# A graph layer and an LSTM on one core: the first stage with its products one line behind, and the first norm's roots as powers on GpSimd

## What is computed

```python
# _layernorm: (x - mean) / sqrt(var + 1e-5), over the 256 features of a node
def gnn(x, src, dst, weight, bias):
    h = x @ weight + bias
    agg = segment_sum(h[src], dst, N)
    deg = maximum(segment_sum(ones, dst, N), 1)
    return agg / deg
x = x + gnn(_layernorm(x), src, dst, gnn_weight, gnn_bias)
# the LSTM runs over the 3125 nodes as one sequence; the state starts at zero
def step(h, c):
    i, o = sigmoid(x_i + h @ V_i), sigmoid(x_o + h @ V_o)
    g = tanh(x_c + h @ V_c)
    c = h * c + i * g
    h = o * tanh(c)
x = x + lstm(_layernorm(x))
```

## Time and profile before

| | before |
|---|---|
| median of 3 runs | 456.59 us (456.39 to 458.94) |
| the profiled execution: time / its span | 457.81 us / 455.9 us |
| busy PE / DVE / ACT / POOL | 416.8 / 341.6 / 321.5 / 145.9 us |
| first stage, to the first sum on PE | 72.82 us |
| granted TensorE clock over the run | 0.983 |

### The profile page before, as it was taken

One profiled execution on the slowest core, in us unless ns is written; L12 is line 12 of the kernel. 1 busy time (PEld: TensorE's weight loads), 2 busy tenths in 40 slices (PEclk: granted clock), 3 DMA queues, 4 the chain that ended last, 5 costly groups with the idle time before them and its releaser, 6 DMA issues.

```text
span 455.9 us, 15425 instructions
## 1 busy us (share of the span) xinstructions
PE 416.8 (91%) x6114; PEld 368.5 (81%) x6114; DVE 341.6 (75%) x1095; ACT 321.5 (71%) x906; POOL 145.9 (32%) x249
## 2 busy tenths in 40 slices
PE   4987899999999999999999999998888889999992
PEld 3666787878898999899998989887777778888882
DVE  4989887996997868777786833627577778888885
ACT  1668696577776767667676853564788888888881
POOL 6740420153432435233422412312123222322320
PEclk9989799999999999999999999999999999999997
DMA  8375001331100001000100010000000000210112
GB/s 186 70 156 140 0 1 51 104 104 31 58 2 1 1 4 55 1 2 1 58 2 1 2 39 20 0 3 22 38 4 4 4 3 4 61 51 12 61 60 62
DMA packets 9603, 16.90 MB, mean 37 GB/s; under 512 B 2006, under 2 KB 7451, under 8 KB 9526
## 3 DMA queue, kind: packets, MB, share of 16 engines
q1 hardware_dynamic: 8230, 14.60, 11.0%
q0 software_dynamic: 880, 0.86, 0.9%
q10 hardware_dynamic: 416, 0.39, 0.5%
HBM read 6.23 MB, written 9.61 MB: 35 GB/s over the span
## 4 chain that ended last, share of the span: by engine, by line
PE 64%; DVE 18%; ACT 7%; issue 7%; DMA 2%; POOL 0%; SPq 0%; DVEq 0%; ACTq 0%; POOLq 0%
PE bank L1244 13%; PE bank L1246 13%; PE bank L1328 10%; PE bank L1436 9%; PE bank L1238 6%; PE bank L1356 4%; ACT tc L1099 3%; PE bank L1278 3%; DVE h L1913 3%; DVE hots L1691 3%; DVE h L1950 3%; DVE c_st L1908 2%; DMA x_sb<-in_x_dram 2%; PE bank L1472 1%; PE bank L1304 1%
## 5 line engine op out<-in xcount | busy, mean ns | idle before, releaser
L1238 PE MATMUL bank<-hots 128*128 128x125 f16 x625 | 119.7, 222 | 0.3 <-DVE hots L1691 0.2
L1691 DVE TENSOR_TENSOR hots<-iota,kp 128x1000 f16<-128x1000 f16 x160 | 106.5, 693 | 12.0 <-PE bank L1238 11.9
L1436 PE MATMUL bank<-h,V 128*128 128x62 f16 (+1 forms) x2952 | 101.1, 192 | 13.0 <-DVE h L1913 8.4
L1436 PEld LDWEIGHTS bank<-h,V 128*128 128x128 f16 x2952 | 93.0, 97 | 24.2 <-issue 22.8
L1244 PE MATMUL bank<-h_flat,counts 125*128 125x257 f16 x375 | 96.7, 273 | 0.2 <-ACT counts L934 0.2
L1246 PE MATMUL bank<-h_flat,counts 125*128 125x256 f16 x375 | 95.8, 271 | 0.0
L934 ACT ACTIVATE counts<-bank 125x500 f16<-125x500 f32 x96 | 55.2, 602 | 20.8 <-PE bank L1238 19.7
L1244 PE MATMUL bank<-h_flat,gx 125*128 125x257 f16 x250 | 68.2, 274 | 0.0
L1246 PE MATMUL bank<-h_flat,gx 125*128 125x256 f16 x250 | 67.5, 270 | 0.0
L824 POOL TENSOR_TENSOR hc<-h_flat,c_st 128x126 f32<-128x126 f32 x80 | 34.0, 425 | 95.7 <-DVE c_st L1908 84.9
L1238 PEld LDWEIGHTS bank<-hots 128*128 128x128 f16 x625 | 57.1, 98 | 7.8 <-DVE hots L1691 0.6
(11 more groups left out here) (185 smaller groups left out, 781.2 us busy)
## 6 DMA issues: line engine op xcount, KB each, us to landing
h_dram<-h_flat SPq DMA_DIRECT2D x1, 3137.2 KB
x_dram<-x_sb SPq DMA_DIRECT2D x5, 625.0 KB
x_sb<-in_x_dram SPq DMA_DIRECT2D x5, 560.0 KB
out_dram<-x_sb SPq DMA_DIRECT2D x4, 560.0 KB
out_dram<-x_sb SPq DMA_DIRECT2D x1, 336.0 KB
x_sb<-in_x_dram SPq DMA_DIRECT2D x5, 65.0 KB
out_dram<-x_sb SPq DMA_DIRECT2D x4, 65.0 KB
gx<-in_L_gnn_weight_dram ACTq DMA_DIRECT2D x1, 256.0 KB, 3.8
```

The source lines that it names most:

```text
L1238: nc.tensor.matmul(ps_count[group % 3][:, pos * KEYS:(pos + 1) * KEYS], hots[:, ring, 0, g // 2, :, g % 2], hots[:, ring, 1, g // 2, 0:KEY ...
L1436: mm = nc.tensor.matmul(to[:, m % (2 * HH) * n:(m % (2 * HH) + 1) * n], V16[:, v_part, d, m * P:(m + 1) * P], h16[:, h_part, d, c0:c1], st ...
L1691: nc.vector.tensor_tensor(hots[:, k % RING, :, :, 0:KEYS, :].rearrange("p a h n g -> p (a h) n g"), iota[:, 0:KEYS, :].unsqueeze(1).to_bro ...
```

## The change

It has four parts.

1. **The roots of the first norm** are powers with exponent -0.5 on POOL (`first_power`): power 0 stands behind the second row fetch, power 1 behind the first edge fetch, power 2 behind the pads, power 3 between POOL's own norms. ACT's square roots, DVE's reciprocals and ACT's later table load (it now loads the tanh table at the start) go.
2. **The first stage's order.** Up to turn 13 products are two lines behind as before; turn 14 does two lines (12 and 13), and from 15 on products are one line behind, so that the loop has 27 turns. From line 14 on the even lines' low parts are DVE's (`low_by_dve`). The second round of keys moves from turns 8 and 11 to 13 and 16; the stats of lines 15 to 24 start one turn earlier; `HOTS_OF` changes; one more one-hot group is written ahead of DVE's last low part. At turn 4 there are 8 unread products instead of 1, and in turns 9 to 16 two of them stand ahead of the transposes.
3. **Second stage**: the first three rests of the weights stand at 69, 74, 79 instead of 64, 71, 77; the last block's root is POOL's, and its transposes stand at place 632 instead of 635.
4. **The test at the end** is six instructions that add the bound, compare and count in one (`test_near`), in place of five in a chain; three of them can start before the last state.

```diff
-            return t >= BLOCKS - 4
+            return t >= CATCH_UP and t % 2 == 0 or t >= BLOCKS - 4
-        PLACE_KEYS, TURN_KEYS = (4, 8), (5, 11)
+        PLACE_KEYS, TURN_KEYS = (4, 13), (5, 16)
-        WARM_TOPS, WARM_FIRST, WARM_EACH = 8, 21, 1
+        WARM_TOPS, WARM_FIRST, WARM_EACH, WARM_KEYS, WARM_END = 8, 21, 1, 8, 17
-        HOTS_OF = [0] * HOTS_FROM + [2, 2, 1, 2, 1, 1, 1] + [2] * 11 + [0]
+        HOTS_OF = [0] * HOTS_FROM + [2, 2, 2, 2, 1, 1, 2, 0] + [2] * 10 + [0]
+        CATCH_UP = PLACE_KEYS[1] + 1
+        LINES_END = BLOCKS + 2
+        def lines_at(j):
+            if j < CATCH_UP:
+                return range(max(0, j - 2), max(0, j - 1))
+            return range(j - 2 if j == CATCH_UP else j - 1, min(j, BLOCKS))
...
+            def first_power(n):
+                j0, j1 = NORMS[n]
+                pool.wait_ge(var_ready, n + 1)
+                nc.gpsimd.tensor_tensor(rstd[:, j0:j1], var_eps[:, j0:j1], minus_half[0:NB, 0:1].to_broadcast([NB, j1 - j0]),
+                                        ALU.pow).then_inc(power_ready, 1)
...
-                nc.scalar.activation(sd[:, j0:j1], var_eps[:, j0:j1], ACT.Sqrt).then_inc(sqrt_ready, 1)
...
-                dve.wait_ge(sqrt_ready, n + 1)
-                done(nc.vector.reciprocal(y, sd[:, js]))
+                dve.wait_ge(power_ready, n + 1)
...
-            for turn in range(BLOCKS - 1):
+            for turn in range(BLOCKS):
...
-            UV_LOW = {64: 0, 71: 1, 77: 2, 128: 3, 152: 4, 165: 5}
+            UV_LOW = {69: 0, 74: 1, 79: 2, 128: 3, 152: 4, 165: 5}
...
-        LAST_AT = {FINISH_AT: (561, 580, 605, 630), NORM_AT: (575, 587, 622, 632), TURN_AT: (576, 588, 625, 635),
+        LAST_AT = {FINISH_AT: (561, 580, 605, 630), NORM_AT: (575, 587, 622, 632), TURN_AT: (576, 588, 625, 632),
...
+            def test_near(new, old, k0, k1, bound):
+                a = near_tests[0]
+                near_tests[0] += 1
+                nc.vector.scalar_tensor_tensor(out=near_hits[:, a, :, 0:k1 - k0], in0=new[:, :, k0:k1], scalar=bound,
+                                               in1=old[:, :, k0 + 1:k1 + 1], op0=ALU.add,
+                                               op1=ALU.is_le if bound < 0 else ALU.is_ge, accum_out=near[:, a:a + 1]
+                                               ).then_inc(near_ready, 1)
```

More of the change, by code:

```diff
@@ L772, in _ @@
             nc.gpsimd.memset(counts[1][:, :, :, NB:P], 0.0).then_inc(pads_set, 1)
-            roots = [1]
-            pool.wait_ge(root_seq, 1)
+            roots = [0]
             def root(turn, j):
@@ L806, in _ @@
                     nc.gpsimd.memset(c_st[:, :, :, :], 0.0).then_inc(e_start, 1)
-                if turn >= 3:
+                if 3 <= turn < BLOCKS - 1:
                     early_old_part(turn - 2)
@@ L941, in _ @@
             act.wait_ge(consts, 1)
-            nc.scalar.activation(sd[0:1, 0:1], ones[0:1, 0:1], ACT.Sqrt).then_inc(table_set, 1)
+            nc.scalar.activation(tc[0:1, 0, 0, 0:1], ones[0:1, 0:1], ACT.Tanh).then_inc(table_set, 1)
             act.wait_ge(scales_ready, 1)
@@ L969, in _ @@
                     counts_out(windows_of(k + 1) - 1)
-                if 0 <= j - 3 and not low_by_dve(j - 3):
-                    line_low(j - 3)
-                if 0 <= j - 2 < BLOCKS:
-                    line_high(j - 2)
+                for t in lines_at(j - 1):
+                    if not low_by_dve(t):
+                        line_low(t)
+                for t in lines_at(j):
+                    line_high(t)
             tile = 0
@@ L1032, in _ @@
                     act.reg_load(gate_scale, w_unscale[0:1, 2:3].bitcast(I32))
-                    nc.scalar.activation(tc[0:1, 0, 0, 0:1], ones[0:1, 0:1], ACT.Tanh).then_inc(table_set, 1)
                 if w in UV_HIGH:
@@ L1480, in _ @@
                         if (step, d) == (STEPS - 1, 1):
-                            pe.wait_ge(near_ready, 1)
-                            nc.tensor.matmul(ps_one[0:1, 0:1], near[:, :], ones[:, 0:1], start=True, stop=True
-                                             ).then_inc(near_ps, 1)
+                            for a in range(NEAR_TESTS):
+                                pe.wait_ge(near_ready, a + 1)
+                                mm = nc.tensor.matmul(ps_one[0:1, 0:1], near[:, a:a + 1], ones[:, 0:1],
+                                                      start=(a == 0), stop=(a == NEAR_TESTS - 1))
+                            mm.then_inc(near_ps, 1)
                         turn_out(step, d, LAST_ROUND + step + 1 - HIDDEN)
@@ L1728, in uv_extreme @@
                 extreme(n, w[:, :, :, :].rearrange("p d n h -> p (d n h)"))
-            for j in range(BLOCKS + 3):
+            for j in range(LINES_END):
                 if j < BLOCKS:
                     zT_low(j)
-                if j >= 3 and low_by_dve(j - 3):
-                    line_low(j - 3)
+                for t in lines_at(j - 1):
+                    if low_by_dve(t):
+                        line_low(t)
                 if j == 0:
@@ L1762, in _ @@
                     uv_extreme(1, U_sb)
-            for k in range(OUTS, FIRST_HOTS):
+                if j == BLOCKS:
+                    one_hots(OUTS)
+            for k in range(OUTS + 1, FIRST_HOTS):
                 one_hots(k)
@@ L2005, in _ @@
                     link(nc.vector.tensor_copy(open_i[:, :], open_f[:, :]))
-            settle()
-            counted_op(nc.vector.tensor_tensor(gap[:, 1, :, :], gap[:, 1, :, :], gap[:, 1, :, :], ALU.mult))
-            for q in range(2):
-                dve.wait_ge(h_ready[q], POST)
-            link(nc.vector.tensor_tensor(gap[:, 0, :, :], h_after(DONE)[:, :, 0:CHUNKS - 1],
-                                         h_start[:, :, 1:CHUNKS], ALU.subtract))
-            link(nc.vector.tensor_tensor(gap[:, 0, :, :], gap[:, 0, :, :], gap[:, 0, :, :], ALU.mult))
-            gap_all = gap[:, :, :, :].rearrange("p a m k -> p (a m k)")
-            nc.vector.scalar_tensor_tensor(out=gap_all, in0=gap_all, scalar=STATE_TOL ** 2,
-                                           in1=ones[:, 0:1].to_broadcast([P, 2 * HH * (CHUNKS - 1)]), op0=ALU.is_le,
-                                           op1=ALU.mult, accum_out=near[:, :]).then_inc(near_ready, 1)
+            test_cells(0, STATE_TOL)
+            test_states(-STATE_TOL)
+            test_states(STATE_TOL)
             for d in range(HH):
```

147 lines of the change are left out of this document (73 added, 74 removed).

## The result

| | before | after |
|---|---|---|
| median of 20 runs each | 457.91 us (456.39 to 459.55) | 459.21 us (456.96 to 461.03) |
| ratio after / before, 95% interval | | 1.0032 (1.0021 to 1.0043) |
| the profiled execution: time / its span | 457.81 / 455.9 us | 457.89 / 456.0 us |
| granted TensorE clock over the run | 0.983 | 0.984 |
| first sum on PE | 72.82 us | 73.75 us |

The changed kernel is 0.3% slower. 451.7 us was forecast, with 449.0 to 456.1 as the range: wrong, and by 7.5 us. About 1.3 us of these are the start of the sum: it stood on the median of three runs, 456.59 us, and that of 20 runs of the same kernel is 457.91. The rest is the change itself, forecast at -4.9 us. Two figures have to be kept apart there: the profiled executions are equal to 0.1 us, and the medians differ by 1.3 us (1.5 by the ratio).

A forecast was written before the change was run, and what follows sets the result against it. DVE was taken to set the first stage's pace, with PE full in half-clock stretches around. Terms -4.1 - 1.0 + 0.8 - 0.6 = -4.9 us took 457.81 to 452.9, less 1.22 to the median: 451.7 us, range 449.0 to 456.1.

The forecast's parts named there:

- the -4.1 us of the first sum: First stage, powers and new order together: first sum on PE at 68.7 us, 4.1 us earlier.
- Powers 0 and 1: First two roots on POOL: 1.12 and 0.51 us later, 1.63 us by the time of the first keys.
- I take 0.92 us for either width: Price of a POOL power of five or ten columns, taken from one-column rows as a fixed cost.
- Power 3: Ten-column power on POOL, mostly covered by a one-hot group and a `zT_low` on DVE; costs 0.2 us.
- ACT's are worth nothing.: Removing ACT's four square roots and table load gains nothing, as neither lies on the chain of waits.
- the clock still falls at the start: Rival, first stage: PE stands longer before the first keys, DVE waits 0.9 us again; 452.6 us, chance 0.15.
- The order: First stage, line 6 to line 17: DVE's waits go, 24.7 us left of 28.20, plus 0.2 for a power.
- The last stretch: From line 17's split to the first sum: PE is the bound, 13.7 us counted from 55.0 us.
- Second stage: PE's 1.01 us wait for the first norm goes, by later weights' rests and an earlier one-hot group: -1.0 us.
- the rival that it swallows a lead: Rival, second stage: DVE, busy without a gap for 30 us, eats the 4.1 us; 455.8 us, chance 0.07.
- Last transposes: End of second stage: PE turns the last norm ahead of the step's products, which start 0.8 us later.
- The rival of the dear powers: Powers cost e us a column beyond 0.19 us, first sum at 65.9 + 20e us; chance 0.11.

The follow-up runs named there:

- e4_last_root_back: Changed kernel with the last root back on VectorE and the last norm's transposes at 635: 457.16 us, 0.9987 of the kernel before.
- e1_sqrt_back: Changed kernel with all four powers undone, square roots on ScalarE and reciprocals on VectorE again: 458.79 us, 1.0020 of the kernel before.
- e11_no_powers: Kernel of e6_best with four square roots and no powers, the fourth at ScalarE's turn 13: 454.90 us, 0.9929 of the kernel before.
- e9_turn_635: Changed kernel with only the last norm's transposes back at place 635: 457.39 us, 1.0013 of the kernel before.
- e3_fillers: Changed kernel with 18 more unread products on TensorE at the start: 459.03 us, 1.0024 of the kernel before.
- e5_two_waits: Changed kernel with the last Newton step a turn later and the last two groups of counts ahead of line 24's products: 458.79 us, 1.0017.
- e10_busy_at_last: Changed kernel with 18 unread products on TensorE ahead of its wait for the last norm: 458.42 us, 1.0024 of the kernel before.
- e6_best: Changed kernel with e5_two_waits' edits, square roots for the first two norms, last root on VectorE, transposes at 635: 453.90 us, 0.9926.

## Why the prediction was wrong, step by step

The term that failed is the -4.1 us of the first sum. At full clock it was -0.5 us (72.36 against 72.82), and the changed kernel's own profile has +0.9. Of the 3.7 us between forecast and full clock 0.5 stand before the split of line 6, 1.9 between that and the split of line 17 (C), and 1.4 behind it (D). The other terms came out near what was said.

- **Powers 0 and 1.** 1.63 us later by the first keys was forecast. The split of line 6 stands at 30.10 us in `e4_last_root_back`, 2.1 us later; in the other kernels with these two powers it is 29.8 to 31.5 us, with A varying by 1.3 us among them. Power 0 was as said: 1.95 us from the variance to Newton's first multiplication in place of 0.95, 1.00 later (1.12 said). Power 1 was mis-sized: 1.22 us for five columns, not 0.92. With the hand-over its root came 0.77 us later, and with the 0.42 us that the keys' instruction took more, B is 1.27 us longer (12.00 or 12.01 us in five kernels against 10.73 or 10.74), not 0.51. The step that failed is "I take 0.92 us for either width": the cost goes by the column, 0.22 us, between my lower bound and the 0.36 of the upper one.
- **Power 3.** 0.2 us was forecast; DVE stood 1.52 us. That is the 2.31 us of the power less the two instructions over it; by "0.92 us for either width" it was the largest single miss, 1.3 us. With the Newton step one turn later the wait is gone at no price (C 25.61 us).
- **"ACT's are worth nothing."** Wrong for one of the four: a square root on ScalarE holds its queue until the variance is there (1.16 us before, 2.00 in `e1_sqrt_back`). The prediction saw this wait in its own list for the order's part and did not book it with the powers. It is the one thing that the runs show the powers to give, and a later place gives it too (`e11_no_powers`).
- **The clock at the start.** The rival "the clock still falls at the start" (0.15) is what the profile shows, and it is near in size: 1.4 us where it had 0.9. That is luck in part, for its cause was not the one seen: it looked at the keys, and the fall came 10 us earlier, behind PE's stand for the first norm. It did not come in every execution: `e4_last_root_back` had none, and `e9_turn_635` a shorter one (0.66 in 18 to 22 us) behind a longer stand (2.34 us). The keys' place was no wrong guess either: in `e3_fillers`, `e5_two_waits` and `e10_busy_at_last` the clock fell behind the keys' stand of 1.5 us.
- **The order.** 24.7 us for C and 0.2 for the power were forecast; at full clock C is 26.8, of which 1.3 is the power and 0.46 a wait for ACT's copy at line 16. That DVE finds "every copy ready" holds but for that one. The half clock went from the middle in this profile, but not from the run: the mean granted clock is 0.985 over the 20 runs of the changed kernel and 0.985 over those of the kernel before. "I take both half-clock stretches as gone" failed; they only stand elsewhere.
- **The last stretch.** From the split of line 17 to the first sum 14.1 us were forecast, and it is 15.47 or 15.48 us in six kernels that differ elsewhere, at full clock. The working took PE as the bound and 0.24 us of waiting as before. PE's own work was near what was said (13.83 us busy), but it stands 0.36 us for ScalarE at 58.9 us and 1.29 us at the end. The loop is one turn shorter, so the last counts now stand behind line 24's products, and ScalarE copies them after that line. The step that failed is taking a last wait over from the old order; moving the counts and their copies ahead of line 24 gave back 0.56 us (`e5_two_waits`, `e6_best`).
- **Second stage.** -1.0 forecast, -0.88 measured, and the rival that it swallows a lead is refuted (`e6_best`). The reason was half right: not the weights' rest (nothing by itself), but what DVE no longer has before it at 100 us: one group of one-hots (0.6 us). The other 0.3 us were not taken apart.
- **Last transposes.** +0.8 forecast, +0.88 measured. Not foreseen: the stand they open can halve the clock for another 1.4 us.
- **Tests.** -0.6 forecast, -0.94 measured. As said, three of the six tests stand ahead of the last state; but that state did not come later (G is the same to 0.01 us), where 0.2 was taken.

At full clock the terms as measured give -0.46 at the first sum (72.36 against 72.82), -0.88, +0.88 and -0.94: 1.4 us faster than before. The medians say 1.3 slower. What lies between is, as far as the profiles show it, the half clock: 1.4 us at the start of the stage (the changed kernel's own profile), 1.3 and 1.6 in C (`e3_fillers`, `e10_busy_at_last`), 1.4 to 1.7 in F (three of five). The mean granted clock of whole runs fits: it is 0.996 in the profiles of `e4_last_root_back` and `e6_best`, which have no fall in the first two stages, and 0.980 to 0.990 in the 20 runs of the changed kernel, so every one of them had falls. Among these 20 a run is 0.17 us shorter for each thousandth of clock more (standard error 0.07); from their mean to 0.996 that makes 1.9 us, an estimate that goes beyond the clocks that were seen. How often each place has its fall stays open, since only the profiled execution shows where the clock fell, and so does the rest of the 2.7 us.

The rival of the dear powers had the price right in kind: its sum, 65.9 + 20e us, gives 70.1 with e = 0.21 as measured, 1.4 us more than the forecast. The first sum at full clock is 72.4; what that sum lacks too are 1.4 us in the last stretch, 0.5 at line 16 and 0.4 before the split of line 6.

## What to carry to other kernels

A price that was seen for one column is no price for ten: where rows have one width only, the estimate should go through both ends, and the slope decides. An instruction moved to an idle engine is cheap only if the result is not awaited at once; what an in-order queue gains from a move may be had by putting the waiting instruction one turn later, as here. When a loop is made a turn shorter, ask anew what stands last in it, on each engine. And a new wait on TensorE can cost more than its own length: the one before the last transposes cost 0.9 us where the clock held and 2.3 to 2.6 where it fell.

## What was not expected of the hardware

- A power on GpSimd goes by columns: 1.22 us for 125x5 and 2.31 us for 125x10. The first power took 1.22 us like the two behind it. The Trainium skill, GPSIMD Engine Reference, section 2.1 "Instruction dispatch", has about 6 us for the first call of freshly loaded code. No run here shows that.
- The same instructions with the same stand had the clock at 1.00 in one execution and at half in another: `e4_last_root_back` and `e10_busy_at_last` have one first stage, TensorE stands 1.5 us before the first keys in both, and behind it the granted clock was 1.00 in the first and 0.50 from 30 to 35 us in the second. The falls of the first two stages came in or behind a stand of TensorE of 0.97 us or more, but not every such stand had one: in the first stages of `e4_last_root_back` and `e9_turn_635` together six of 1.4 to 1.9 us passed at full clock.
